# A two-layer decoder: expert weight copies shared with GpSimd, and the end of the last layers in another order

## What is computed

```
x = ln(x + attention(x))            # 16 heads of 64, causal
x = ln(x + cross_attention(x, ctx))
x = ln(x + moe(x))                  # 8 experts, top 2, 256 -> 2*512 -> 256
x = ln(x + gated_block(x))          # 16 heads of 16, cumulative gates, rope, its own MLP 256 -> 1024 -> 256
x = ln(x + cross_attention(x, ctx)) # 4 heads of 64
x = ln(x + channel_mix(x))
# expert:       (min(g,9) * sigmoid(1.702 g)) * (clip(v,-9,9) + 1), then W2
# channel mix:  xr, xk = x shifted by one token, mixed by mu_r, mu_k
#               sigmoid(xr Wr) * (relu(xk Wk)**2 Wv)
```

## Time and profile before

| | us |
|---|---|
| median of 3 runs | 1354.98 |
| the profiled execution | 1355.9 |
| its span, first to last instruction | 1354.0 |
| TensorE busy | 1137.6 (84%) |
| VectorE busy | 735.5 (54%) |
| ScalarE busy | 574.0 (42%) |
| GpSimd busy | 415.8 (31%) |
| mean granted TensorE clock | 0.942 |

### The profile page before, as it was taken

The page is one execution under the profiler, slowest core; times in us unless marked ns, Lnnn a source line. Parts: engine busy times, 40 slices in busy tenths (PEclk is TensorE's granted clock), DMA queues, the critical chain, the costliest instruction groups (busy, mean ns, idle before and its releaser), DMA issues. The chain is left out here.

```text
span 1354.0 us, 20004 instructions
## 1 busy us (share of the span) xinstructions
PE 1137.6 (84%) x6714; PEld 788.5 (58%) x6714; DVE 735.5 (54%) x2208; ACT 574.0 (42%) x1389; POOL 415.8 (31%) x509
## 2 busy tenths in 40 slices
PE   7889989988998877999999553795998998897886
PEld 3456456445644656988988422552654664565665
DVE  1472475358237535555555328575667659554255
ACT  1371263237125512444444153554575465543432
POOL 0250042016003665444444325124122322302111
PEclk9999999999999996999999876897998998998898
DMA  5000200020010134511111251001000100000000
GB/s 185 16 1 1 54 17 1 0 69 1 1 53 1 51 119 137 179 40 48 48 40 48 77 169 31 1 0 32 9 0 0 32 24 1 0 2 23 0 1 31
DMA packets 40224, 52.35 MB, mean 39 GB/s; under 512 B 10780, under 2 KB 33372, under 8 KB 40124
## 3 DMA queue, kind: packets, MB, share of 16 engines
q1 hardware_dynamic: 31100, 36.66, 8.6%
q0 software_dynamic: 3408, 9.31, 2.4%
q10 hardware_dynamic: 5616, 5.11, 1.2%
HBM read 41.76 MB, written 9.31 MB: 38 GB/s over the span
## 5 line engine op out<-in xcount | busy, mean ns | idle before, releaser
L1256 PE MATMUL bank<-words 128*128 128x256 f32 (+3 forms) x848 | 282.9, 487 | 37.2 <-ACT words L1754 19.0
L1256 PEld LDWEIGHTS bank<-words 128*128 128x128 f32 (+1 forms) x848 | 165.6, 202 | 130.5 <-issue 70.0
L358 PE MATMUL bank<-words 128*128 128x512 f32 x384 | 172.8, 601 | 8.3 <-DMA words<-in_wq 8.3
L324 POOL TENSOR_TENSOR words<-words 128x256 f32<-128x256 f32 (+1 forms) x128 | 103.6, 831 | 190.0 <-DVE words L700 190.0
L855 PE MATMUL bank<-words 128*128 128x128 f32 x1248 | 151.7, 281 | 8.4 <-ACT words L889 6.7
L855 PEld LDWEIGHTS bank<-words 128*128 128x128 f32 x1248 | 144.8, 194 | 22.8 <-ACT words L889 22.7
L571 ACT ACTIVATE words<-words 128x128 f32<-128x128 f32 (+1 forms) x256 | 113.3, 444 | 50.1 <-DVE words L695 50.1
L904 ACT ACTIVATE words<-words 128x2048 f32 x39 | 74.5, 1911 | 131.4 <-issue 131.4
L358 PEld LDWEIGHTS bank<-words 128*128 128x128 f32 x384 | 72.4, 193 | 90.4 <-issue 89.8
L553 ACT ACTIVATE words<-bank 128x512 f32<-128x512 f32 x48 | 28.7, 598 | 192.2 <-PE bank L358 192.2
L610 DVE COPY words<-bank 128x512 f32<-128x512 f32 x48 | 33.2, 691 | 105.9 <-PE bank L358 105.7
(11 more groups left out here) (259 smaller groups left out, 1997.8 us busy)
## 6 DMA issues: line engine op xcount, KB each, us to landing
words<-in_w SPq DMA_DIRECT2D x8, 1024.0 KB, 10.8
y_slots<-words ACTq DMA_DIRECT2D x39, 128.0 KB, 1.7
words<-in_w SPq DMA_DIRECT2D x8, 512.0 KB, 11.2
words<-in_xt SPq DMA_DIRECT2D x4, 512.0 KB, 4.0
words<-in_x SPq DMA_DIRECT2D x4, 512.0 KB, 4.3
x_rows<-words SPq DMA_DIRECT2D x16, 128.0 KB, 1.8
words<-in_wm SPq DMA_DIRECT2D x2, 1024.0 KB, 6.6
out_x<-words SPq DMA_DIRECT2D x16, 128.0 KB, 1.8
```

Source lines behind the costliest of these rows:

```text
L324: last = pool.tensor_tensor(part, part, inv[:, j % SLOTS0, :, t:t + 1].to_broadcast([P, 2, P * (t + 1)]), ALU.mult)
L358: last = pe.matmul(bank[c % 2][:, :], w, r, start=k == 0, stop=k == KD - 1)
L1256: last = pe.matmul(out, w, r, start=i == 0, stop=i == len(pairs) - 1)
```

## The change

1. Expert stage. ACT copies only the gate half of a tile's weights (2 pieces of 512 words), and now waits for `upgate`. POOL copies the value half (`copy_values`) after it has issued the gather of the same tile; it reads the owner's number itself, waits for `ready` while experts still arrive, and for `upvalue` of tile j-2. PE waits for `vcopied` ahead of the value half.
2. End of the last layers. The second older query product moves behind the last group's output products; rows of the MLP are copied ahead of both exponentials; the older group's second scores use banks 1 and 3, and both halves stand together; the up products use more banks (`LASTUP`), the four down tiles have a bank each (`LASTDOWN`), so their waits are gone. The older receptance and its tanh come early, ahead of the last group's keys; its keys of the mix and its values are put between the last group's attention steps; relu and square of the older mix are both on DVE, as are the copies of the last group's values `vx`. Results and normalisations of the last mix alternate by batch.

The diff's core follows; in the written-out orders (PE, ACT, DVE from `older_queries(0)` on) the removed lines are left out.

```diff
+        def halves(weights, half):
+
+            return weights.rearrange("p (k n) -> p k n", k=KD)[:, :, half * FF:(half + 1) * FF]
...
+            def copy_values(j):
+
+                e = pool.value_load(owneri[0:1, j:j + 1], min_val=0, max_val=NE - 1)
+                if j < ARRIVING:
+                    pool.wait_ge(ready, e + 1)
+                    pool.sem_inc(alone, 1)
+                elif j == ARRIVING:
+                    pool.wait_ge(ready, NE)
+                if j >= 2:
+                    pool.wait_ge(upvalue, j - 1)
+                pool.tensor_copy(halves(wfix[:, j % 2, :], 1), halves(w1[:, bass.ds(e * W1, W1)], 1)).then_inc(vcopied, 1)
...
             for j in range(SLOT_TILES):
                 if j + 2 < SLOT_TILES:
                     pool.wait_ge(rturned, j + 1)
                     gather(j + 2)
+                    copy_values(j + 2)
                 pool.wait_ge(gated, j + 1)
                 pool.tensor_tensor(sig[:, :], gate[:, :], sig[:, :], ALU.mult).then_inc(mixed, 1)
...
                     pe.wait_ge(wcopied, j + 1)
+                else:
+                    pe.wait_ge(vcopied, j + 1)
...
-                    act.wait_ge(upvalue, j - 1)
-                act.activation(wfix[:, j % 2, :], w1[:, bass.ds(e * W1, W1)], ACT.Copy).then_inc(wcopied, 1)
+                    act.wait_ge(upgate, j - 1)
+                act.activation(halves(wfix[:, j % 2, :], 0), halves(w1[:, bass.ds(e * W1, W1)], 0), ACT.Copy).then_inc(wcopied, 1)
...
+        LASTUP, LASTDOWN = ((4, 5, 0, 2), (1, 3, 4, 5)), (0, 2, 1, 3)
...
-            rstd(OTHER, n8, 0)
-            rstd(OTHER, n8, 1)
             for b in range(2):
                 rstd(LAST, n7, b)
                 last_difference(b)
+            for b in range(2):
+                rstd(OTHER, n8, b)
...
+            def older_receptance(b):
+
+                for i in range(HALF):
+                    last = product(both(4 + b, b)[:, i, :], [(xr[:, k, tok(HALF * b + i)], wr[:, k, :]) for k in range(KD)])
+                last.then_inc(rmm, 1)
+
+            def older_values(b):
+
+                for i in range(HALF):
+                    last = product(both((3, 1)[b], b)[:, i, :], [(rl[:, k, tok(HALF * b + i)], wv2[:, k, :]) for k in range(KD)])
+                last.then_inc(n8.product, 1)
+
...
+            older_queries(0)
             for t in range(NT):
                 pe.wait_ge(ogc, 2 * LAST + t // HALF + 1)
                 if t >= 2:
                 else:
                     pe.wait_ge(ogr, NT * LAST + NT)
                 product(bank[t % 2][:, 0:D], [(ogt[:, k, tok(t)], wout[:, k, :]) for k in range(KD)]).then_inc(n5.product, 1)
+            older_queries(1)
             turn(LAST, n5, 0, lambda t: h5[:, t, :], bank[2])
             pe.wait_ge(n5.copied, 2 * LAST + 1)
             last_up(0, 0)
+            turn(LAST, n5, 1, lambda t: h5[:, t, :], bank[2])
+            pe.wait_ge(xqr, KD * OTHER + KD)
+            context_scores(OTHER, 0)
+            pe.wait_ge(n5.added, NT * LAST + NT)
+            context_scores(OTHER, 1, (1, 3))
             last_up(0, 1)
             last_up(0, 2)
+            pe.wait_ge(n5.copied, 2 * LAST + 2)
             last_up(0, 3)
+            context_turn(OTHER, 0, (6, 7))
+            context_turn(OTHER, 1, (6, 7))
+            pe.wait_ge(xe, GB * OTHER + GB)
             last_up(1, 0)
             last_up(1, 1)
+            context_turn(OTHER, 2, (6, 7))
+            context_turn(OTHER, 3, (6, 7))
+            pe.wait_ge(m1gelu, 2)
             last_up(1, 2)
             last_up(1, 3)
             pe.wait_ge(xtc, NT * OTHER + NT)
             for q in range(GB * KD):
                 context_sums(OTHER, q)
+            pe.wait_ge(m1gelu, MC // 2)
+            last_down(0)
             pe.wait_ge(xz, 4 * OTHER + 4)
             for t in range(NT):
                 context_product(OTHER, t)
             last_down(1)
             pe.wait_ge(n7.added, NT * OTHER + NT)
             for b in range(2):
                 turn(OTHER, n7, b, lambda t: x(OTHER, t), bank[6 + b])
             pe.wait_ge(m1gelu, MC)
+            last_down(2)
+            last_turn(n6, 0, bank[0])
+            last_down(3)
+            pe.wait_ge(mixed, 2 * OTHER + 1)
+            older_receptance(0)
+            older_receptance(1)
             pe.wait_ge(loaded, 32 * LAST + 32)
+            pe.wait_ge(n6.copied, 2 * LAST + 1)
             for c in range(KD):
                 product(bank[2 * c][:, 0:GB * S2], [(wxk[:, k, tok(c)], memt[:, k, :]) for k in range(KD)]).then_inc(xkm, 1)
+            last_turn(n6, 1, bank[1])
+            pe.wait_ge(n6.added, NT * LAST + NT)
+            last_queries(0, 3)
+            last_queries(1, 1)
             pe.wait_ge(xkr, KD * LAST + KD)
             pe.wait_ge(n7.copied, 2 * OTHER + 2)
             pe.wait_ge(lastxqr, 1)
             context_scores(LAST, 0)
+            pe.wait_ge(lastxqr, 2)
+            context_scores(LAST, 1, (0, 2))
+            for b in range(GB):
+                pe.wait_ge(rsig, NT * OTHER + b + 1)
+                product(bank[4 + b][0:S2, 0:D], [(memt[:, k, b * S2:(b + 1) * S2], wxv[:, k, :]) for k in range(KD)]).then_inc(xvm, 1)
             pe.wait_ge(mixed, 2 * OTHER + 2)
+            for c in range(KD):
+                product(bank[3 - 2 * c][:, :], [(wk2[:, k, tok(c)], xk[:, k, :]) for k in range(KD)]).then_inc(kmm, 1)
+            pe.wait_ge(lastvr, GB)
+            context_turn(LAST, 0, (4, 5), lastsm)
+            context_turn(LAST, 1, (4, 5), lastsm)
             pe.wait_ge(kact, KD * OTHER + KD)
+            older_values(0)
             pe.wait_ge(xtc, NT * LAST + 2)
             context_sums(LAST, 0, (6, 7), lastpxt)
             context_sums(LAST, 1, (6, 7), lastpxt)
+            context_turn(LAST, 2, (4, 5), lastsm)
+            context_turn(LAST, 3, (4, 5), lastsm)
             pe.wait_ge(xz, 4 * LAST + 2)
             context_product(LAST, 0)
             context_product(LAST, 1)
             pe.wait_ge(xtc, NT * LAST + NT)
+            context_sums(LAST, 2, (0, 2), lastpxt)
+            context_sums(LAST, 3, (0, 2), lastpxt)
+            older_values(1)
+            last_turn(n7, 0, bank[4])
             pe.wait_ge(xz, 4 * LAST + 4)
+            context_product(LAST, 2, (0, 2))
+            context_product(LAST, 3, (0, 2))
+            last_turn(n7, 1, bank[5])
+            last_mix(0, 6, 7)
+            last_values(0, 4)
+            last_mix(1, 0, 2)
+            last_values(1, 5)
...
+            older_queries_copy(0)
+            mlp_rows(LAST, 0, 2)
+            older_queries_copy(1)
+            mlp_rows(LAST, 1, 2)
             context_exp(OTHER, 0)
+            context_exp(OTHER, 1, (1, 3))
             act.preload_act_table_set("gelu_and_others")
+            last_gelu(0, 0)
+            context_copy(OTHER, 0, 6)
+            context_copy(OTHER, 1, 7)
+            last_gelu(0, 1)
+            context_copy(OTHER, 2, 6)
+            context_copy(OTHER, 3, 7)
+            last_gelu(0, 2)
+            last_gelu(0, 3)
             for i in range(MC // 2):
+                last_gelu(1, i)
             for q in range(GB * KD):
                 sums_copy(OTHER, q)
             for b in range(2):
                 mix_rows(OTHER, b, 6 + b)
+            last_rows(0, 0)
+            for b in range(2):
+                act.wait_ge(rmm, NT * OTHER + b + 1)
+                act.activation(rs[:, rows_of(b), :], both(4 + b, b), ACT.Tanh, scale=0.5).then_inc(rsig, 1)
             for c in range(KD):
                 act.wait_ge(xkm, KD * LAST + c + 1)
                 act.activation(kxt[:, c, :], bank[2 * c][:, 0:GB * S2], ACT.Copy).then_inc(xkr, 1)
+            last_rows(1, 1)
+            last_queries_copy(0, 3)
+            last_queries_copy(1, 1)
             act.preload_act_table_set("natural_log_exp_and_others")
             context_exp(LAST, 0, sm=lastsm)
+            context_exp(LAST, 1, (0, 2), lastsm)
+            context_copy(LAST, 0, 4, lastpxt)
+            context_copy(LAST, 1, 5, lastpxt)
             act.preload_act_table_set("gelu_and_others")
             sums_copy(LAST, 0)
             sums_copy(LAST, 1)
+            context_copy(LAST, 2, 4, lastpxt)
+            context_copy(LAST, 3, 5, lastpxt)
+            sums_copy(LAST, 2, (0, 2))
+            sums_copy(LAST, 3, (0, 2))
+            mix_rows(LAST, 0, 4)
+            mix_rows(LAST, 1, 5)
             last_activations(0, 6, 7)
+            last_activations(1, 0, 2)
...
+                if banks == (6, 7):
+                    together = psum[:, 512 * 6:512 * 8].rearrange("p (o n) -> p o n", o=2)[:, :, 0:4 * S2].rearrange("p o (h n) -> p o h n", n=S2)
+                    dve.tensor_reduce(xmax[:, b, :].rearrange("p (o h) -> p o h", o=2), together, AX.X, ALU.max)
+                else:
+                    for o in range(2):
+                        dve.tensor_reduce(xmax[:, b, :].rearrange("p (o h) -> p o h", o=2)[:, o, :], logits[o], AX.X, ALU.max)
...
+            for t in range(3):
```

(47 more changed lines are left out.)

152 lines of the change are left out of this document (15 added, 137 removed).

## The result

| | before | after |
|---|---|---|
| median on one chip, us | 1354.95 (4 runs, 1352.31 to 1355.09) | 1323.15 (4 runs, 1322.31 to 1324.78) |
| ratio, 95% interval | | 0.9766, 0.9752 to 0.978 |
| profiled execution, its span | 1355.9, 1354.0 | 1322.73, 1320.7 |
| mean granted TensorE clock | 0.942 | 0.946 |

The change makes the kernel 31.8 us faster; 28.6 were forecast. The three parts of the program can be told apart by two points that both traces have: the last down product of the expert stage (761.47 before, 745.59 after) and the first query product of the end (1225.01 before, 1207.99 after). The expert stage gives 15.9 us, the stages between, which nobody touched, 1.1, and the end 16.3 (129.0 to 112.7); the sum is the 33.3 us between the spans.

A forecast was written before the change was run, and what follows sets the result against it. ScalarE's loop was taken to bound the expert stage, TensorE's gaps the end. Gains of 15.4 + 13.2 = 28.6 us bring the median from 1354.98 to 1326.4 us, range 1320 to 1341.

The forecast's parts named there:

- ScalarE's loop: Expert stage: 5.87 us a tile, falling to 5.00 with the half copy, below TensorE's 5.52; gain 15.4 us.
- X = 1.75: Expert stage: X is the time GpSimd's value-half copy takes, estimated 1.05 us; 0.7 us slack makes about 1.75 free.
- Rival 2: Expert stage: GpSimd's copy runs at the two-input rate, 14.5 us of gain gone, 1340.9 us; chance 0.12.
- rival 4: Expert stage: GpSimd's round becomes the bound; kernel slower from a copy time of 2.7 us, up to 1439; chance 0.04.
- The walk through the end: End: new order stepped through with old durations; last mix 17.4 us earlier, some given back, 15.6 us stay.
- VectorE's receptance mix behind GpSimd's difference: End: the mix waits for GpSimd's difference and holds the last group's second sum; TensorE gap of 3.3 us.
- The end's 13.2 us: End: predicted net gain after clock loss; bounds 15.6 without clock loss and 7.2 with three gaps at 2.8.
- clock reserve: End: 2.4 us taken off for slow TensorE clock behind two gaps over 3 us, 1.0 and 1.4.
- the gaps at 1272 and 1312: End: TensorE gaps of 3.3 and 3.1 us, before the turns of the last group and of batch 1's rows.
- Rival 1: End: the clock takes the gain, three gaps at 2.8 us, 6.0 more, 1332.4 us; chance 0.18.
- Rivals 2, 3, 4: The third: GpSimd's loop replaces ScalarE's and VectorE's later order eats the end's gain, 1355 us; chance 0.04.
- the rule for two inputs: Expert stage: two-SBUF-input VectorE and SBUF-reading GpSimd instructions exclude each other; a meeting would make the copy 1.74 us.

The follow-up runs named there:

- e9: Changed kernel with one more 512-element GpSimd copy into spare words, without drain: 1325.2 us, ratio 0.9772 to the kernel before.
- e10: Changed kernel with one more 1024-element GpSimd copy into spare words, without drain: 1328.16 us, ratio 0.98 to the kernel before.
- e3: Changed kernel with GpSimd's copy of the value half done twice, with a drain between: 1362.87 us, ratio 1.0052 to the kernel before.
- e5: Changed kernel with the last group's second sum, root and first normalisation ahead of receptance mix and GpSimd's difference: 1322.81 us, ratio 0.9755 to the kernel before.
- second run: The changed kernel measured again unaltered, on another chip: 1325.73 us, ratio 0.9776 to the kernel before.

## Why the prediction was right, and where its sizes were off

- **ScalarE's loop was the bound, TensorE is next.** Right: 5.52 us a tile; 15.9 us for 15.4. The half copy on ScalarE takes 1.06 (1.04 forecast), GpSimd's 1.035 (1.05).
- **Up to X = 1.75 costs nothing.** Right: e9 and e10 put the limit between 1.6 and 2.0 (1.035 and the delays of 0.56 and 0.99). GpSimd's own round was mis-sized by the register read of 0.67 us, which costs nothing there; nothing hung on it. Rival 2 rested on a wrong reading: 2.35 us isn't what all two-input operations of 1024 elements took, others in the same trace took 2.00 (894.34) and 1.89. The point of rival 4, 2.7, wasn't measured exactly; at 3.3 the kernel is slower.
- **The walk through the end.** The order of the waits was right, and the times met, in us from the first query product (forecast, trace): first up 8.9, 8.7; older group's turn 42.8, 42.6; last group's first turn 50.8, 50.5, with its gap 3.3, 3.44; last mix 91.7, 91.3; last mix to the end of the last normalisation 19.5, 19.1. But that the last mix was met to 0.4 us is partly luck. The walk had no clock loss in it, and the trace has 1.7 us of it ahead of the mix; without it, as in e3, the mix starts at 89.6. So the walk's steps up to the mix were 2.1 us too long in sum, most of it behind the last group's first turn, and the loss that stood in another term covered it.
- **VectorE's receptance mix behind GpSimd's difference** was the cause of that gap: e5 takes 2.46 of the 3.44 us away by turning the order round. What stayed, 0.98, was no step of mine: VectorE held up by GpSimd. I had looked for such a meeting only at the weight copy, where there was none, and not at the large GpSimd operations of the end.
- **The end's 13.2 us** is the term that was mis-sized, the walk's 15.6 more than the clock reserve of 2.4. I took 1.0 and 1.4 behind the gaps at 1272 and 1312. Behind the first the clock did fall (0.64, in the window shown) and cost 1.7, all of which reached the last mix; behind the second it did not, and cost 0. The end gave 16.3 where I had 15.6 without clock loss and 13.2 with it, so the walk itself was 2.4 too pessimistic: without the 1.7 the end would have given 18.0. In the second run the second loss was there, 1.4 of TensorE's time, and the last mix to the end of the last normalisation took 20.3 us instead of 19.1 (20.9 forecast with the mix slowed). Each loss is one of two outcomes and not a constant: in e3 the first was 0 and the second there. Of the 3.1 us that the end gave beyond the forecast of 13.2, 2.4 are the walk's and 0.7 the reserve's.
- **Rival 1** (the clock takes 6.0 more): no gap cost more than 1.7. **Rivals 2, 3, 4**: GpSimd's copy isn't at the two-input rate, and both parts give what they were to give.
- **Between the stages** 1.1 us came that no step has, in code that is the same; between the traces this stretch takes from 461.4 us (e9) to 468.3 (e5), so 1.1 can't be told from how it varies.

The Trainium skill (SBUF — State Buffer, Who interferes with whom) says that a VectorE instruction in its 2-port mode, which it names `tensor_scalar` for, and a GpSimd instruction lock each other out for a whole instruction. The traces agree where GpSimd starts first, 2.30 and 2.40 us against 0.73 when kept apart; which mode the instruction ran in no row shows. I had weighed only the rule for two inputs beside it.

## What to carry to other kernels

Bound the unknown operation from both sides and compute from which size on it decides; here the room of 0.7 us said in advance that the copy could be shared at no cost. Before adding a filler operation to an experiment, look at what its synchronisation costs. When a short operation on the critical path takes two or three times its usual time, look at what the other engine started within 0.1 us of it: starting that one 0.8 us later closed two gaps of 1.6 us in all here. A forecast that is met at a late point doesn't show that the steps before it were right: here a clock loss of 1.7 us and steps 2.1 us too long stood against each other.

## What the runs showed of the hardware

- GpSimd copies 1024 fp32 elements a partition in 1.035 us and 512 in 0.61: an estimate from these two is 0.83 ns an element and 0.2 us to start; its product of two 512-element inputs takes 1.26.
- While a GpSimd operation on two SBUF inputs runs (1.9 to 2.0 us), VectorE's normalisation from SBUF to SBUF that starts 0.07 us later takes 1.6 us longer: its first tile ends 0.15 us after GpSimd's operation. GpSimd isn't slowed. Behind each other, two such operations held up both tiles (4.50 us for the pair).
- A drain on GpSimd between a copy and the next, with a gather issued ahead, took 0.7 to 2.8 us the first time (4.4 and 4.1 in two tiles at the start) and 0.13 the second.
- The granted clock behind a gap isn't a function of the gap: 2.91 us cost 0 and 1.4 us in two runs of one kernel, 3.44 us cost 1.7 in the changed kernel and 0 in e3, whose end is the same, and 1.58 us cost 0 and 1.7 in two kernels.
